# Another table of thirds for the attention stage of a Mamba and gated feed-forward layer

## What is computed

```python
q = (x @ Wq.T).reshape(b, s, H, HD)          # x: rms-normed rows; 16 heads of 32
k = (x @ Wk.T).reshape(b, s, H, HD)
v = (x @ Wv.T).reshape(b, s, H, HD)
scores = jnp.einsum('bqhd,bkhd->bhqk', q, k) / np.sqrt(HD).astype(np.float32)
probs = jax.nn.softmax(jnp.where(causal, scores, min), axis=-1)
out = jnp.einsum('bhqk,bkhd->bqhd', probs, v).reshape(b, s, d)
attn = out @ Wo.T
mod = MOD_SCALE * jnp.tanh(attn @ A)         # A: 512 x 16
gate_pre = h @ W_in_base.T + mod * (h @ A) @ B
x = x + s * silu(ffn(...))                   # s: the scan's result
```

## Time and profile before

| | |
|---|---|
| median of 3 runs | 2724.37 us |
| profiled execution | 2724.37 us, span 2722.6 |
| mean granted clock of TensorE | 0.964 |
| busy over the span | PE 93%, DVE 52%, ACT 39%, POOL 13% |
| attention, periods 1 to 8 | 982.8 to 1598.9 us; periods start at 982.8, 1070.6, 1149.0, 1227.0, 1305.1, 1383.1, 1460.7, 1537.1 |
| DMAs of the attention loop | QS and KS 384 each of 64 KB, issued by SyncE; x rows 1 MB a batch; RH and RL 1 MB each a batch |

### The profile page before, as it was taken

How to read it: one execution, slowest core, us unless ns; L and a number is a source line. 1 busy time by engine, 2 the same in 40 slices (tenths; PEclk the granted TensorE clock), 3 DMA queues, 4 the chain that set the end, 5 groups by cost and what they waited for, 6 DMA issues and landing times.

```text
span 2722.6 us, 38755 instructions
## 1 busy us (share of the span) xinstructions
PE 2519.8 (93%) x14359; PEld 2025.3 (74%) x14359; DVE 1418.0 (52%) x2943; ACT 1075.1 (39%) x1770; POOL 365.4 (13%) x353
## 2 busy tenths in 40 slices
PE   5899999999997579999999979999999999999997
PEld 3678778778776457777777658888888788888886
DVE  6666566566564358888888854111111513333333
ACT  4444444444442237777777752111111311111111
POOL 0000000000001223443433220000000001111111
PEclk8899999999999589999999969999999999999999
DMA  4000000000001353444444412111111412222212
GB/s 133 16 16 16 32 16 16 32 16 16 16 16 39 119 139 82 128 130 128 131 129 113 128 57 85 50 46 49 47 47 61 153 51 93 93 93 93 93 62 78
DMA packets 97727, 194.59 MB, mean 71 GB/s; under 512 B 22128, under 2 KB 22640, under 8 KB 91376
## 3 DMA queue, kind: packets, MB, share of 16 engines
q1 hardware_dynamic: 97280, 191.78, 22.4%
q10 hardware_dynamic: 256, 0.26, 0.0%
HBM read 99.43 MB, written 41.94 MB: 52 GB/s over the span
## 4 chain that ended last, share of the span: by engine, by line
PE 76%; DVE 8%; SPq 5%; issue 3%; ACT 3%; POOL 3%; DMA 2%; DVEq 0%; POOLq 0%; ACTq 0%
PE PS L72 13%; PE PS L74 13%; PE PS L73 13%; SPq L1362 5%; PE PS L1844 4%; PE PS L1846 4%; PE PS L1845 4%; PE PS L695 2%; PE PS L693 2%; PE PS L694 2%; PE PS L1454 2%; PE PS L1435 2%; DMA STGB<-in_x_dram 2%; PE PS L1411 1%; PE PS L679 1%
## 5 line engine op out<-in xcount | busy, mean ns | idle before, releaser
L1893 DVE TENSOR_TENSOR GF<-SG,PS 128x512 f32<-128x512 f32 x128 | 88.0, 687 | 618.9 <-PE PS L74 618.8
L1630 DVE CUSTOM_DVE_ANT_0 PS<-PS,MK 128x512 f32<-128x512 f32 (+3 forms) x512 | 243.6, 505 | 122.9 <-PE PS L1435 121.8
L1867 ACT ACTIVATE SG<-PS 128x512 f32<-128x512 f32 x128 | 76.3, 596 | 430.0 <-PE PS L1826 430.0
L1545 ACT ACTIVATE PF<-PS 128x512 f32<-128x512 f32 (+1 forms) x384 | 199.5, 527 | 106.4 <-PE PS L1456 87.4
L1871 ACT CAST GH<-GF 128x512 fp32r<-128x512 f32 x128 | 79.3, 620 | 362.7 <-DVE GF L1893 362.7
L72 PE MATMUL PS<-XH,WH 128*128 128x512 f32 x512 | 211.6, 413 | 6.4 <-DVE XC L967 6.4
L72 PE MATMUL PS<-FH,GW 128*128 128x512 f32 x512 | 200.3, 391 | 7.7 <-DVE DW L1888 7.7
L1924 POOL TENSOR_SCALAR XN<-XT,MEAN,RSTD 128x512 f32<-128x512 f32 x32 | 67.7, 2118 | 1040.1 <-DMA M<-m_scratch 726.4
L1844 PE MATMUL PS<-DW,GH 128*128 128x512 f32 x512 | 200.3, 391 | 3.9 <-DVE GL L1895 3.9
L74 PE MATMUL PS<-XH,WL 128*128 128x512 f32 x512 | 202.7, 396 | 0.0
L73 PE MATMUL PS<-XL,WH 128*128 128x512 f32 x512 | 201.7, 394 | 0.0
(11 more groups left out here) (277 smaller groups left out, 5845.9 us busy)
## 6 DMA issues: line engine op xcount, KB each, us to landing
QS<-QT SPq DMA_DIRECT2D x384, 64.0 KB, 2.0
KS<-QT SPq DMA_DIRECT2D x384, 64.0 KB, 2.0
FH<-rh_scratch SPq DMA_DIRECT2D x16, 1024.0 KB, 5.5
FL<-rl_scratch SPq DMA_DIRECT2D x16, 1024.0 KB, 7.7
XF<-in_x_dram SPq DMA_DIRECT2D x32, 256.0 KB, 3.5
s_scratch<-ZS SPq DMA_DIRECT2D x8, 1024.0 KB, 4.3
STGB<-in_x_dram SPq DMA_DIRECT2D x8, 1024.0 KB, 6.8
rh_scratch<-RH SPq DMA_DIRECT2D x8, 1024.0 KB, 8.6
```

Of the source, the lines that this page charges most:

```text
L1545: act.activation(PE_[u][:, o:o + at], PS[4 + a % 2][:, 0:at], ACT.Exp, scale=SC).then_inc(a_ex, 1)
L1630: dve.tensor_tensor_reduce(out=p[:, at:at + n], in0=p[:, at:at + n], in1=MK[:, 512 - n:512], scale=1.0, scalar=NEG, op0=ALU.add, op1=ALU.m ...
```

## The change

It alters numbers in the table, two waits, and on which third three ScalarE entries stand.

- scaled: from thirds 10, 22, 31, 40 to 26, 29, 32, 35 of the period.
- normal of 128-column blocks 2 and 3: from thirds 1 and 2 to 0 and 1 (0 and 1 of the four stay in 46 and 47 of the period before); project now waits for all four low parts ahead of its first step, where steps waited for one part each.
- project: groups from 4-7/8-11, 13-16/20-23, 24-27/29-32, 33-36/38-41 to 3-6/8-11, 14-17/20-23, 25-28/31-34, 36-39/42-45 (q/k).
- values: from 14, 17, 26, 35 to 14, 16, 25, 27; low_rank from 44 to 38. The ScalarE part of both now stands one third behind the matmuls, as values_split and low_rank_out.
- largest_in of a batch's third group from third 19 to 18, in bank 1 instead of 0, with the fourth in bank 0 as before; the modulation's four entries one third earlier, from 11 to 10 on.

```diff
-            for k, third in enumerate((-38, -26, -17, -8)):
-                at(t + third, "scaled", b, k)
-            for d, third, bank in ((0, -2, 0), (1, -1, 1), (2, 1, 0), (3, 2, 1)):
+            for k in range(4):
+                at(t - 22 + 3 * k, "scaled", b, k)
+            for d, third, bank in ((0, -2, 0), (1, -1, 1), (2, 0, 0), (3, 1, 1)):
...
-            for r, q, k in ((0, 4, 8), (1, 13, 20), (2, 24, 29), (3, 33, 38)):
+            for r, q, k in ((0, 3, 8), (1, 14, 20), (2, 25, 31), (3, 36, 42)):
...
-            for J, third in enumerate((14, 17, 26, 35)):
+            for J, third in enumerate((14, 16, 25, 27)):
                 bank_of["values", b, J] = 1
                 at(t + third, "values", b, J)
-                at(t + third + 1, "values_low", b, J)
+                at(t + third + 1, "values_split", b, J)
             bank_of["low_rank", b] = 1
-            at(t + 44, "low_rank", b)
-            for w, third, bank in ((4 * b, 42, 0), (4 * b + 1, 54, 1), (4 * b + 2, 67, 0), (4 * b + 3, 78, 0)):
+            at(t + 38, "low_rank", b)
+            at(t + 39, "low_rank_out", b)
+            for w, bank in ((4 * b, 0), (4 * b + 1, 1), (4 * b + 2, 1), (4 * b + 3, 0)):
                 bank_of["largest_in", w] = bank
-                at(t + third, "largest_in", w)
-                at(t + third + 1, "largest_out", w)
+                at(12 * w - 6, "largest_in", w)
+                at(12 * w - 5, "largest_out", w)
...
-            at(t + 107, "modulation", b)
+            at(t + 106, "modulation", b)
...
                     if k == 0:
                         own01(kind, a, n)
+                        pe.wait_ge(a_rl, 4 * (a // 4) + 4)
                         pe.wait_ge(a_pd, 35)
-                    if a % 4 == n == 0:
-                        pe.wait_ge(a_rl, 4 * (a // 4) + k + 1)
```

## The result

The changed kernel takes 2752.69 us (median of four runs, 2752.31 to 2753.7), the kernel before 2724.98 (2722.7 to 2726.91): 1.0103 times as long, 95% interval 1.0085 to 1.012. The forecast had the sign (+6.7 us), not the size (+28), and 2752.7 lies outside its range.

The account below looks back on a forecast made before the run. TensorE was taken to bound the kernel, busy 74 of about 78 us a period. Full periods +14.4, first -8.5, seventh +1.3, tail -0.5: total +6.7 us on 2724.37, so 2731, range 2712 to 2743.

Parts of the forecast that it names:

- the stop of third 15: First period: GpSimd's scaling waits for a late load; moving it removes 11.6 us plus 0.8 of slow clock, later periods 0.9.
- SyncE stayed off the path: Copies for a group take 16.7 us, start at the same thirds, six thirds ahead of need; no cost.
- new bank chain: PSUM banks 0 and 1 pass between users within one or two thirds, before three; all new waits sum to 9.2 us a period.
- term for third 33: Mixture waits for GpSimd's queue of values, sums, scaling and remainder: 0.9 us a period, bounds 0 to 1.7.
- thirds 18 and 30: Maxima transposes wait for banks held by late values (third 18, 1.2 us) and the q projection's drain (third 30, 1.1 us).
- AM in third 10: Modulation transpose, one third earlier, waits for the sum it reads: 1.0 us a period.
- the sign that the mixture would no longer lead the waits of TensorE: Transposes of maxima waiting for V, for QT, and of AM would lead TensorE's waits instead.
- a slow clock behind the ten idle microseconds: First period, third behind third 15: TensorE at 1.2 GHz for a while, 2.29 us instead of 1.47; 0.8 us go.
- Rival C: Later of scaling and VectorE remainder stands still, three scalings a period; mixtures late; 11.5 us a period, 2745 us; chance 0.09.
- Rival A: Old waits go, new chains mostly hidden: 4.5 us a period gives about 2702, 6.5 about 2714; chance 0.27.
- late maxima copy in the first period: Maxima copy of third 19 falls into the 3 MB transfer: +0.4 us.

## Why the prediction was right and wrong

Right: the stop of third 15 went whole (13.47 to 1.89 us, and with it 0.9 a period later; removing only that is worth 17 us), SyncE stayed off the path (scores wait 0.2 us in all for its copies), and each new bank chain cost what the chain of traced durations gave. Without the scalings in the wrong place the changed kernel stands at the time before; the forecast less its term for third 33 (0.9 in each of six periods) says 2725.6, and 2725.8 was measured; that they meet within 0.2 is in part luck, as single runs of that kernel go from 2721.9 to 2729.9. The casts of ScalarE are shown to be the reason in thirds 18 and 30, and AM in third 10.

The step that failed is the term "Third 33": the chain was right, and its durations were too small. It started right (VectorE's values ended 12.4 us after the start of third 24, forecast 12.3), then added "a second sum (0.7), a scaling (2.07, the clean value) and the remainder (0.65)". The same paragraph quoted 1.56 and 3.04 for such instructions and kept them for the bound. With the lengthened values the term would have been 0.9+0.86+0.24+0.70 = 2.7; 2.9 was measured. The bound of 1.7 held about one lengthening, though three instructions in a row could each meet a VectorE instruction in a queue that never rests. So the sign that the mixture would no longer lead the waits of TensorE failed too.

The second part of the miss is the clock. The forecast charged a slow clock behind the ten idle microseconds of the earlier trace rows and nowhere else; here 2.8 idle microseconds were enough in four of six periods, at about 1.5 us each (83.3 to 84.8).

The account of the 21.0 us between forecast and result: each of five full periods is 3.3 longer than forecast (2.0 at third 33, 0.9 of clock, since it falls in three of the five, 0.3 of the rest), the first period 3.3, the seventh 1.1.

Rival C had the mechanism at 0.09, and the wrong place and price: it charged scalings beside VectorE's remainder 1.0 each, at thirds 33, 36 and 39. In the changed kernel scalings were lengthened by 0.24 in six of 24 cases. What is lengthened are the values' second operation (0.67 to 1.72 us, in 14 of 28, in none of before), the second sum (to 1.56, in before too) and GpSimd's remainder (mean 0.94 instead of 0.74); thirds 36 and 39 have no stop of their own. Rival A, nearly three in ten, was far off: no new wait was hidden. The 0.4 us that the forecast put on a late maxima copy in the first period did not come: its thirds 18 to 32 are as long as those of the fifth, to 0.01 us.

Open: why the clock fell in four periods and not in two, after stops of the same length. The run with the maxima moved had shorter stops (2.5 us) and the clock fell after every one, so the length of the stop alone does not settle it. No run varies only that.

## What to carry to other kernels

Where instructions of two engines exclude each other, as here, price a queue at the lengthened durations once it has no slack: count the partner's instructions that will meet it, not the clean length. A move that helps in one order (these scalings: -17 us) costs in another (27 us): cost each edit against the queue that the other edits make. For a bank that changes hands, follow the drain of the bank that is entered as well as of the one that is left, and remember that an early engine standing idle at its entry may be free (the values cast), while one placed behind a long cast is not.

## What the runs showed of the hardware

- VectorE's remainder and a GpSimd instruction reading SBUF delay each other. Where VectorE came first, GpSimd's went from 0.67 to 1.72 and from 0.70 to 1.56 us, and ended about 0.5 us after VectorE's; where a GpSimd sum came first, VectorE's went from 1.21 to 1.71. A GpSimd scaling that came 0.23 us first cost VectorE only 0.40 us of the 1.84 that it still ran. Over the kernel GpSimd was busy 402 us instead of 365 with the same 353 instructions.
- TensorE fell to 1.2 GHz after stops of 2.8 us in third 33 (four of six), back at 2.4 GHz by third 36 or 37, and after stops of 2.5 us in third 19 in another kernel (seven of seven), back by third 22. After stops of 1.1 us and less in third 33 it stayed at 2.4.
